# More groups of unread matmuls in the cross-attention units of a fused decoder layer, and another table of them for its last two units

## The chip, the cores and the metric

The kernel runs on one core of one Trainium2 chip. The metric is device time in microseconds (us), the median of several runs. Matmuls and weight loads run on TensorE (PE and PEld in the profile), row maxima and small vector work on VectorE (DVE), exponentials and copies out of PSUM on ScalarE (ACT), elementwise work between SBUF buffers on GpSimd (POOL). SyncE (SP) issues nearly all DMAs.

## The reference

One pre-norm decoder layer over 8 batches of 512 tokens of width 256, 16 heads of width 16:

```python
x = x + attn(layernorm(x), ...)            # rotary self-attention
x = x + xattn(layernorm(x), ctx, ...)      # causal self-attention plus cross-attention, summed, one projection
x = x + ffn(layernorm(x), Wg, w1, w2)      # 16 experts, top 1, capacity 256 tokens each

# xattn
y = softmax(mask(q @ k.T * scale)) @ v                       # causal
y = y + softmax(qc @ kc.T * scale) @ vc                      # against the context
# ffn
gate = softmax(x @ Wg); idx = argmax(gate)
loc = running position of each token within its expert; valid = loc < C
h = relu(dispatched @ w1); out = h @ w2; combined = out[idx, loc] * gate * valid
```

## The kernel before, in words

The attentions are cut into **units**, one attention of one batch each: eight of kind A (rotary, n = 0 to 7), then kind B (causal) and kind C (cross) in turn (B for n = 8, 10, ... 22 and C for n = 9, 11, ... 23). Two units before them only prepare (n = -2, -1), and one behind them (n = 24) only finishes. The units from n = 10 to 21 are the bodies of a loop. A unit with `route=True` also normalises, gates and scatters a finished batch to its expert: those are the **routing units**, n = 11, 13, ... 23, which are all of kind C, and n = 24. Behind the units stand the 16 experts.

Each unit has 32 **slots**, and the order of every engine's work in a slot is written out by hand. On TensorE a slot t is, in this order:

- the product of exponentials and values of three slots back (line 741, tile psO);
- `maxima()`: the scores of 12 slots ahead, query by key, into psS (line 764, for causal ones the masks at lines 772 and 776). DVE takes their negated row maxima (line 1193). psS has three banks, so line 764 waits for the maxima of the slot before (`max_done`). From slot 20 on these scores belong to the next unit;
- `exponents()`: the scores of this slot, key by query, into psK (line 795), with two extra rows that carry the maxima. ACT takes their exponentials (line 1029). Every eighth slot (0, 8, 16, 24) begins a new group of heads, and there line 795 first waits for the DMA that brought the group's maxima (`negmax_in_0` or `negmax_in_1`);
- at slots in the table `WARM_JOB`, some unread matmuls;
- the **jobs** that a table gives this slot: transposes and projections for the unit after the next, values for the next one, output projections, and in routing units two transposes (zT at slots 20 and 21, line 831), the gate's logits (slot 22, line 880) and the counts (slot 25, line 888). They share one bank, psM;
- at slots in the table `WARM_END`, some unread matmuls.

An **unread matmul** (`keep_warm`, line 693) multiplies the first 128 columns of a weight matrix by 512 of its columns into a psK bank that nothing reads before it is overwritten. In `exponents()` the group stands between the scores for the maxima and the wait for the group's maxima, at slot 0 in units A and C and slot 16 in units B:

```python
need(pe, s["exp_done"], b.at("exp_done", w - 1))
keep_warm(psK[:, banks[0], :], b.warm_rows.get(t, 0))
if t % 8 == 0:
    pe.wait_ge(s[f"negmax_in_{g % 2}"], b.at(f"negmax_in_{g % 2}", (0, 32, 32, 64)[g]))
```

The groups of the two tables go to the psK bank that this slot does not use, and wait until all exponentials of the slot before are done.

The normalisation of a routing unit runs on DVE in slot 14 (the small operations of lines 1147 to 1157) and, after one power on POOL (line 1427), in slots 18 and 19 (line 1165). In C units POOL multiplies the result of the attention before by its reciprocal sums (line 1473) once these have come by DMA. The program asks for it in slot 11.

Of the kernel before, what the change touches and what calls it, by code (L numbers as in the profile page):

```python
# [86 lines left out]
            "back": 15, "out": 14},  # L87
}
WARM_JOB = {"A": {5: 2, 7: 2}, "C": {25: 2}}
WARM_END = {"AA": {6: 2}, "AB": {6: 2, 7: 2}, "BB": {6: 2, 7: 2, 30: 2}, "CC": {12: 3, 15: 2}}  # L90
NO_ROW = 65536
NEG = -1e30
LN_EPS = 1e-5
# [7 lines left out]
class Body:  # L101


    def __init__(self, kind, prev, nxt, nx2, n, dn=0, route=False):
        self.kind, self.prev, self.nxt, self.nx2, self.route = kind, prev, nxt, nx2, route
        self.parity = n % 2
        self.fin = prev if prev in ("A", "C") else None
        self.form = "first" if n == -2 else "second" if n == -1 else "end" if kind is None else "A" + nx2 if kind == "A" else kind + kind
        self.slots = SLOTS_OF[self.form]
        self.attn_slot, self.recip_slot, self.norm_slot = (self.slots.get(k) for k in ("attn", "recip", "norm"))  # L110
        self.scatter_slots, self.route_steps, self.chain_slots = (self.slots.get(k, ()) for k in ("scatter", "route", "chain"))
        self.ln_steps, self.load_slots = self.slots.get("ln", ()), self.slots.get("load", ())
        self.warm_job = WARM_JOB.get(kind, {})
        self.warm_end = WARM_END.get(self.form, {})
        self.warm_rows = {16: 3} if kind == "B" else {0: 3}
        self.n, self.dn, self.ahead = n, dn, None
        self.base, self.stride, self.i = {}, {}, 0

# [1483 lines left out]
```

## Time and profile before

| what | value |
|---|---|
| median of 3 runs | 1646.93 us (1642.42 to 1662.5) |
| the profiled execution | 1641.89 us |
| its span (first to last recorded instruction) | 1640.1 us |
| mean granted TensorE clock | 0.965 of full speed |
| TensorE busy (matmuls) | 1443.4 us, 88% of the span |
| VectorE busy | 1211.1 us, 74% |
| ScalarE busy | 1064.8 us, 65% |
| GpSimd busy | 648.6 us, 40% |

The profiled execution is one more run; its time lies 1.79 us above its span. A granted clock of 1.00 is 2.4 GHz and one of 0.50 is 1.2 GHz; a stretch that was at both levels shows a mean. "Idle before" is time in which an engine had nothing running just before an instruction, with what released it behind the arrow.

In the times below, the group of unread matmuls at slot 15 of unit n = 11 starts at 703.57 us.

### The profile page before, as it was taken

How to read it: one execution, taken by the hardware profiler on the slowest of the kernel's cores; microseconds unless marked ns; L12 is line 12 of the kernel's file. 1: busy time of each engine (PE TensorE's matmuls, PEld its weight loads, DVE VectorE, ACT ScalarE, POOL GpSimd, SP SyncE). 2: the span in 40 equal slices, each digit the busy share in tenths (PEclk: the TensorE clock that was granted, in tenths of full speed). 3: DMA queues.
4: the chain of work that ended last, by engine and by line, in shares of the span. 5: the costliest groups of instructions: out<-in, count | busy, mean ns of one | idle time of the engine just before them, and what ended most of it. 6: DMA issues, size and time to landing. Idle time of an engine off the chain costs nothing.

```text
span 1640.1 us, 37863 instructions
## 1 busy us (share of the span) xinstructions
PE 1443.4 (88%) x14610; PEld 650.8 (40%) x14610; DVE 1211.1 (74%) x2434; ACT 1064.8 (65%) x2139; POOL 648.6 (40%) x535
## 2 busy tenths in 40 slices
PE   3799999999999898988988889989889888779997
PEld 1222333332333434334334234334343332259987
DVE  6788878878776776877877877777768677537774
ACT  2477778778777677656766666666767656425652
POOL 2544565456422423226235234342351311225554
PEclk9799999999999999989999999899999999899999
DMA  6445344433323333323323323332233221157771
GB/s 178 114 123 136 110 117 122 118 104 105 90 74 89 99 100 97 94 72 101 89 81 78 100 68 80 99 89 70 80 96 89 67 55 42 48 183 253 255 262 62
DMA packets 119480, 175.82 MB, mean 107 GB/s; under 512 B 26274, under 2 KB 85896, under 8 KB 114697
## 3 DMA queue, kind: packets, MB, share of 16 engines
q1 hardware_dynamic: 111376, 158.50, 34.1%
q0 software_dynamic: 5888, 14.24, 2.6%
q8 instruction: 108, 1.77, 0.5%
q10 hardware_dynamic: 2048, 0.83, 0.2%
q14 instruction: 60, 0.48, 0.1%
HBM read 102.33 MB, written 51.18 MB: 94 GB/s over the span
## 4 chain that ended last, share of the span: by engine, by line
PE 54%; DVE 18%; DMA 9%; ACT 6%; issue 6%; POOL 5%; SPq 2%; POOLq 0%; DVEq 0%; ACTq 0%
PE psO L741 13%; PE psM L466 10%; PE psS L764 9%; DVE negmax L1193 9%; PE psK L466 6%; PE psK L795 6%; ACT probs L1029 4%; PE psS L466 4%; DMA recipB<-recip_scratch 3%; PE psK L693 2%; DMA shared<-shared 1%; DVE xn L1165 1%; PE psM L831 1%; PE psM L880 1%; DMA stack<-mrows 1%
## 5 line engine op out<-in xcount | busy, mean ns | idle before, releaser
L1193 DVE TENSOR_REDUCE negmax<-psS 128x1 f32<-128x512 f32 (+3 forms) x1536 | 869.5, 615 | 266.4 <-PE psS L764 136.0
L1029 ACT ACTIVATE probs<-psK 128x512 f32<-128x512 f32 (+3 forms) x1536 | 753.6, 544 | 306.8 <-PE psK L795 182.7
L741 PE MATMUL psO<-probs,V 128*32 128x256 f32 (+1 forms) x5632 | 444.5, 388 | 21.2 <-ACT U L1021 15.1
L764 PE MATMUL psS<-stack 48*128 48x512 f16 (+3 forms) x1536 | 285.0, 367 | 62.6 <-DVE negmax L1193 57.4
L795 PE MATMUL psK<-stack 50*128 50x512 f16 (+3 forms) x1536 | 278.9, 359 | 23.6 <-DMA stack<-mrows 14.6
L764 PEld LDWEIGHTS psS<-stack 48*128 48x128 f16 x1536 | 74.4, 93 | 377.7 <-DVE negmax L1193 298.8
L741 PEld LDWEIGHTS psO<-probs,V 128*32 128x32 f32 x5632 | 113.3, 108 | 207.8 <-issue 116.3
L795 PEld LDWEIGHTS psK<-stack 50*128 50x128 f16 x1536 | 76.4, 95 | 55.5 <-ACT probs L1029 20.9
L1427 POOL TENSOR_TENSOR rstd<-lnt,minus_half 128x4 f32<-128x4 f32 x24 | 24.6, 1026 | 157.9 <-DVE lnt L1157 157.9
L1553 POOL DMA_INDIRECT out_dram<-stack,put_to x32 | 76.7, 2398 | 17.9 <-issue 9.1
L1441 POOL CAST shared<-shared 128x512 f16<-128x512 f32 x8 | 4.9, 610 | 191.2 <-ACT shared L1051 191.2
L466 PE MATMUL psM<-xT,wx 128*128 128x512 f16 x288 | 74.1, 385 | 5.0 <-POOL xT L1443 2.5
L1443 POOL TENSOR_TENSOR parts<-shared,parts 128x512 f16<-128x512 f32 x64 | 74.0, 1156 | 5.1
L1441 POOL CAST parts<-shared 128x512 f16<-128x512 f32 x64 | 39.1, 612 | 89.4 <-ACT shared L1063 89.4
L831 PE MATMUL psM<-consts,xn 128*128 128x128 f32 x184 | 31.9, 299 | 42.6 <-DVE xn L1165 29.3
L1021 ACT COPY U<-psO 128x512 f32<-128x512 f32 x96 | 56.8, 592 | 15.1 <-PE psO L741 14.6
L693 PE MATMUL psK<-wo 128*128 128x512 f16 x224 | 65.5, 386 | 0.5
L1063 ACT ACTIVATE shared<-psM,bias_qk 128x512 f32<-128x512 f32 x64 | 44.2, 691 | 21.6 <-PE psM L466 21.6
L1473 POOL TENSOR_TENSOR recipB<-packed,recipB 128x1024 f32<-128x1024 f32 x15 | 35.3, 2351 | 57.1 <-DMA recipB<-recip_scratch 57.1
L772 PE MATMUL psS<-halves 64*128 64x128 bf16 x512 | 57.5, 221 | 0.0
L1521 POOL TENSOR_TENSOR shared<-rs,gate_scale 128x4 f32<-128x4 f32 x8 | 1.6, 205 | 139.7 <-DVE scatter_to L1365 139.7
L807 PE MATMUL psK<-halves 64*128 64x128 bf16 x512 | 55.9, 214 | 0.0
(192 smaller groups left out, 2071.3 us busy)
## 6 DMA issues: line engine op xcount, KB each, us to landing
spare<-in_L_ffn_w_dram SPq DMA_DIRECT2D x32, 1024.0 KB, 6.3
parts_scratch<-parts SPq DMA_DIRECT2D x192, 128.0 KB
stack<-parts_scratch SPq DMA_DIRECT2D x96, 256.0 KB, 4.1
stack<-parts_scratch SPq DMA_DIRECT2D x96, 128.0 KB, 4.0
packed<-U SPq DMA_DIRECT2D x192, 64.0 KB
recipB<-recip_scratch SPq DMA_DIRECT2D x48, 256.0 KB
shared<-shared SPq DMA_DIRECT2D x48, 128.0 KB, 2.1
probs<-back_scratch POOLq DMA_DIRECT2D x16, 258.0 KB, 3.2
```

What stands on the lines that cost most here:

```text
L466: mm = nc.tensor.matmul(out, left(x, k), right(y, k), start=(k, x, y) == steps[0], stop=(k, x, y) == steps[-1])
L693: nc.tensor.matmul(out, wo1[:, 0, 0, 0:P], wo1[:, 0, :, :], start=True, stop=True, skip_group_check=True)
L741: mm = nc.tensor.matmul(psO[32 * i:32 * i + 32, q0:q1], v_of(par)[:, kt, 2 * g + i % 2 + PAIRS * (i // 2), :], probs[:, (unit + i % 2) % P ...
L764: mm = nc.tensor.matmul(psS[:, banks[hh], 0:n], stack_of(par, 0)[rows, hp, qt * P:(qt + 1) * P], stack_of(par, 1)[rows, hp, 0:n], start=Tr ...
L772: nc.tensor.matmul(psS[:, banks[hh], n - P:n], unit_a[rows, :], mask_q[rows, :], start=False, stop=False, skip_group_check=True)
L795: mm = nc.tensor.matmul(psK[:, banks[hh], q0:T], stack_of(b.parity, 1)[rows, hp, kt * P:(kt + 1) * P], stack_of(b.parity, 0)[rows, hp, q0: ...
L807: mm = nc.tensor.matmul(psK[:, banks[hh], q0:q0 + P], unit_b[rows, :], mask_k[rows, :], start=False, stop=True, skip_group_check=True)
L1021: nc.scalar.copy(U[:, g % 2, :], psO[:, :]).then_inc(s["av_out"], 1)
L1029: nc.scalar.activation(probs[:, t % P_RING, i, q0:T], psK[:, S_BANKS[t][i], q0:T], ACT.Exp, scale=SM_SCALE / (1 if b.kind == "A" else WSCA ...
L1193: nc.vector.tensor_reduce(negmax[:, g % 2, at:at + 1], psS[:, S_BANKS[u // 2][j], 0:n], AX_X, ALU.max, negate=True).then_inc(s["max_done"], 1)
L1443: nc.gpsimd.tensor_tensor(lo, src, hi, ALU.subtract).then_inc(s[lo_done], 1)
L1553: nc.gpsimd.indirect_dma_start(out=out_rows_dram, out_offset=bass.IndirectOffsetOnAxis(ap=put_to[:, c, st:st + 1], axis=0), in_=eo_sb[c][: ...
```

## The change

Two tables and one selection are edited:

```diff
-WARM_END = {"AA": {6: 2}, "AB": {6: 2, 7: 2}, "BB": {6: 2, 7: 2, 30: 2}, "CC": {12: 3, 15: 2}}
+WARM_END = {"AA": {6: 2}, "AB": {6: 2, 7: 2}, "BB": {6: 2, 7: 2, 30: 2}, "CC": {12: 3, 15: 2, 21: 2},
+            "last": {15: 2, 22: 2}}
...
-        self.warm_end = WARM_END.get(self.form, {})
-        self.warm_rows = {16: 3} if kind == "B" else {0: 3}
+        self.warm_end = WARM_END.get("last" if kind and nx2 is None else self.form, {})
+        self.warm_rows = {"B": {16: 3}, "C": {0: 3, 16: 3}}.get(kind, {0: 3})
```

- Every C unit (eight of them, n = 9 to 23) gets three unread matmuls at slot 16, ahead of the wait for the third group's maxima.
- The C units n = 9 to 21 (seven) get two behind the jobs of slot 21, and these wait until the exponentials of slot 20 are done. In the six routing units among them that is between the second transpose zT and the logits. Unit n = 9 does not route, and its slot 21 has only the transpose of maxima.
- The last two units, n = 22 (B) and n = 23 (C), have nothing more to prepare (`nx2` is None) and get a table of their own. Unit n = 22 loses its groups at slots 6, 7 and 30 (six matmuls) and gets groups at 15 and 22 (four). Unit n = 23 loses the group of three at slot 12, keeps the one at 15 and gets one of two at 22, behind the logits.

Over the run that is 24 + 14 - 2 - 1 = 35 matmuls more. Every line behind the tables moves down by one, so line 795 is 796 afterwards.

TensorE in unit n = 11, slots 15 to 17, before (psO is the product with the values, psS the scores for the maxima, psK from `stack` the scores for the exponentials, psK from `wo` the unread group):

```order
L693 MATMUL psK<-wo 128x512 [waits exp_done]
L693 MATMUL psK<-wo 128x512
L741 MATMUL psO<-probs,V 32x256 x4
L764 MATMUL psS<-stack 128x512 [waits max_done]
L764 MATMUL psS<-stack 128x512
L795 MATMUL psK<-stack 128x512 [waits negmax_in_0,exp_done]
L795 MATMUL psK<-stack 128x512
L741 MATMUL psO<-probs,V 32x256 [waits exp_done]
```

and the same place now:

```order
L694 MATMUL psK<-wo 128x512
L742 MATMUL psO<-probs,V 32x256 x4
L765 MATMUL psS<-stack 128x512 [waits max_done]
L765 MATMUL psS<-stack 128x512
L694 MATMUL psK<-wo 128x512 [waits exp_done]
L694 MATMUL psK<-wo 128x512 x2
L796 MATMUL psK<-stack 128x512 [waits negmax_in_0]
L796 MATMUL psK<-stack 128x512
L742 MATMUL psO<-probs,V 32x256 [waits exp_done]
```

The three new ones stand behind the wait for `max_done` and ahead of the one for `negmax_in_0`.

TensorE in unit n = 11, slots 21 and 22, before (psM from `xn` is the transpose zT, from `negmax` the transpose of the maxima):

```order
L795 MATMUL psK<-stack 128x512 [waits exp_done]
L795 MATMUL psK<-stack 128x512
L867 MATMUL psM<-consts,negmax 16x128 [waits max_done,zT_out]
L831 MATMUL psM<-consts,xn 128x128 [waits ln_out,negmax_rows]
L831 MATMUL psM<-consts,xn 128x128 x3
L741 MATMUL psO<-probs,V 32x256 x4
L764 MATMUL psS<-stack 128x384 [waits max_done]
```

and now:

```order
L832 MATMUL psM<-consts,xn 128x128 [waits ln_out,negmax_rows]
L832 MATMUL psM<-consts,xn 128x128 x3
L694 MATMUL psK<-wo 128x512 [waits exp_done]
L694 MATMUL psK<-wo 128x512
L742 MATMUL psO<-probs,V 32x256 x4
L765 MATMUL psS<-stack 128x384 [waits max_done]
```

The pair comes after the transpose that waits, and before the product of slot 22, its scores and the logits.

TensorE in unit n = 22, slots 15 and 16, now (the first of the groups is new, the second stood there before):

```order
L796 MATMUL psK<-stack 128x128 x2
L804 MATMUL psK<-halves 128x64 x2
L808 MATMUL psK<-halves 128x128 x2
L694 MATMUL psK<-wo 128x512 x2
L742 MATMUL psO<-probs,V 32x256 x4
L765 MATMUL psS<-stack 128x128 x2
L773 MATMUL psS<-halves 128x128 x2
L777 MATMUL psS<-halves 128x64 x2
L694 MATMUL psK<-wo 128x512 x3
L796 MATMUL psK<-stack 128x512 x2
```

Here line 796 with `psK<-stack 128x512` waits for the third group's maxima.

## Rows read from the trace of the kernel before

**Rows 1.** The page: span, engines, granted clock in 40 slices, chain by engine.
```profile
span 1640.1 us, 37863 instructions
PE 1443.4 (88%) x14610; PEld 650.8 (40%) x14610; DVE 1211.1 (74%) x2434; ACT 1064.8 (65%) x2139; POOL 648.6 (40%) x535
PEclk9799999999999999989999999899999999899999
PE 54%; DVE 18%; DMA 9%; ACT 6%; issue 6%; POOL 5%; SPq 2%; POOLq 0%; DVEq 0%; ACTq 0%
```

**Rows 2.** Groups by line: count, busy us, mean ns, idle before, by releaser.
```profile
L1193 DVE TENSOR_REDUCE negmax<-psS 128x1 f32<-128x512 f32 (+3 forms) x1536 | 869.5, 615 | 266.4 <-PE psS L764 136.0 <-PE psS L776 124.9 <-issue 0.3
L764 PE MATMUL psS<-stack 48*128 48x512 f16 (+3 forms) x1536 | 285.0, 367 | 62.6 <-DVE negmax L1193 57.4 <-DMA stack<-parts_scratch 1.3
L693 PE MATMUL psK<-wo 128*128 128x512 f16 x224 | 65.5, 386 | 0.5
```

**Rows 3.** Timeline, line 693: start, us; three at half clock, three at full clock.
```profile
68.88 1.46 PE L693 MATMUL psK<-wo 128*128 128x512 f16 x3
697.50 0.81 PE L693 MATMUL psK<-wo 128*128 128x512 f16 x3
```

**Rows 4.** Slot 15 to next slot 6, n=11 to 21: length; PE, PEld, DVE, ACT, POOL; PEclk.
```profile
703.57:749.44 45.87, 38.53 (x441) 16.89 (x440) 31.25 (x81) 28.57 (x59) 17.49 (x18) 0.89 0.27 80
818.29:861.48 43.19, 35.63 (x442) 15.20 (x440) 31.23 (x85) 28.68 (x59) 16.12 (x18) 0.96 0.27 79
932.03:976.89 44.86, 36.92 (x441) 15.21 (x440) 31.73 (x85) 28.72 (x59) 16.61 (x18) 0.92 0.26 77
1045.54:1090.17 44.63, 39.51 (x441) 17.70 (x439) 29.41 (x85) 28.36 (x59) 13.70 (x16) 0.85 0.26 76
1159.95:1199.84 39.89, 34.16 (x441) 15.13 (x440) 29.15 (x82) 28.37 (x59) 13.59 (x15) 1.00 0.29 83
1269.52:1313.01 43.49, 35.67 (x442) 15.05 (x440) 30.45 (x80) 28.61 (x59) 17.27 (x18) 0.96 0.24 70
```

**Rows 5.** Timeline around slot 16 of unit n = 11, last row n = 15.
```profile
703.29 2.35 POOL L1473 TENSOR_TENSOR shared<-packed,recipB 128x1024 f32<-128x1024 f32 x1 [7.29 <-DMA recipB<-recip_scratch]
703.31 2.35 DVE L1152 TENSOR_SCALAR lnt<-lnt 128x4 f32<-128x4 f32 x1
706.88 0.40 PE L764 MATMUL psS<-stack 48*128 48x512 f16 x2 [2.15 <-DVE negmax L1193]
709.29 1.29 DVE L1193 TENSOR_REDUCE negmax<-psS 128x1 f32<-128x512 f32 x2 [0.67 <-PE psS L764]
...
936.07 0.61 PE L764 MATMUL psS<-stack 48*128 48x512 f16 x2 [2.88 <-DVE negmax L1193]
```

**Rows 6.** Timeline from slot 16 to 20 of unit n = 17.
```profile
1046.32 4.87 DVE L1193 TENSOR_REDUCE negmax<-psS 128x1 f32<-128x512 f32 x8
1047.06 0.39 PE L764 MATMUL psS<-stack 48*128 48x512 f16 x2 [0.35 <-DVE negmax L1193]
1054.56 0.63 PE L831 MATMUL psM<-consts,xn 128*128 128x128 f32 x4 [1.44 <-DVE xn L1165]
```

**Rows 7.** Stretches as in Rows 4: units n = 11 (four), n = 17, n = 23.
```profile
703.70:707.10 3.40, 1.25 (x13) 0.36 (x12) 3.37 (x5) 0.98 (x2) 3.32 (x3) 1.00 0.27 83
707.10:710.50 3.40, 3.40 (x24) 0.53 (x20) 2.73 (x5) 1.87 (x4) 3.32 (x5) 0.51 0.35 105
717.40:720.80 3.40, 1.99 (x23) 1.07 (x23) 1.01 (x4) 1.73 (x5) 0.00 (x0) 1.00 0.09 31
720.80:727.60 6.80, 6.80 (x48) 4.25 (x47) 2.84 (x9) 2.37 (x5) 0.00 (x0) 0.50 0.10 23
...
1055.30:1068.90 13.60, 12.29 (x85) 6.42 (x77) 4.23 (x12) 4.74 (x10) 0.00 (x0) 0.50 0.11 30
...
1389.80:1396.60 6.80, 6.80 (x40) 4.14 (x44) 2.38 (x11) 2.60 (x6) 0.00 (x0) 0.50 0.09 21
```

**Rows 8.** Timeline of slots 21 and 22 of unit n = 11.
```profile
718.85 0.66 PE L831 MATMUL psM<-consts,xn 128*128 128x128 f32 x4 [1.41 <-DVE mrows L1296]
720.58 3.44 PE L880 MATMUL psM<-wg,shared 128*128 128x16 f32 x16
```

**Rows 9.** Timeline, slot 16 of unit n = 22.
```profile
1328.62 0.61 PE L795 MATMUL psK<-stack 50*128 50x512 f16 x2 [2.44 <-DMA stack<-mrows]
```

## The prediction

> **What bounds the kernel now.** I read the page first. TensorE is busy 88% of the span and carries 54% of the chain that ended last, DVE another 18%; the granted clock is full in nearly all slices [rows 1]. So what is added on TensorE is paid unless something there was idle anyway, and a better clock can give back little. The groups by line then show how the two engines hang together: before the scores for the maxima (line 764) TensorE sits idle 62.6 us in all, 57.4 of them for DVE's maxima, and DVE sits idle 266.4 us, nearly all for TensorE's scores [rows 2]. They hand three banks back and forth, so a delay of one soon becomes a delay of the other.
>
> The place of the change is read by comparing like with like. Six routing C units run the same instructions from slot 15 to slot 6 of the next unit, and take 39.89 to 45.87 us [rows 4]. Unit n = 19, at a clock of 1.00 throughout, is the fastest. Two things make the others longer. One is a stall of TensorE at slot 16. In n = 11 POOL's product (line 1473) started as its DMA landed, at 703.29, and a small DVE operation begun at the same moment took 2.35 us, as long as the product; behind it TensorE waited 2.15 us for the maxima, and in n = 15 2.88 [rows 5]. Two more such rows, in units 13 and 21, have 2.38 and 2.27 us. Units 17 and 19 do not: in n = 17 the wait at that place is 0.35 us [rows 6]. The other is the clock at 1.20 GHz, its lower level. In n = 11 it was full up to 707.1, the stretch with the stall, and low in the 3.4 us behind it; full while zT waited for its bank and low for 6.8 us behind that, with the logits in it [rows 7, 8]. In n = 17 it was low for 13.6 us.
>
> The price of a low clock follows from n = 17, which has no stall: 44.63 - 39.89 = 4.74 us longer, at a mean clock of 0.85, which is 2 x 0.15 x 44.63 = 13.4 us at the lower level. That is **0.35 us lost per microsecond of low clock**. A cross-check on n = 11: stall 2.15 and 2 x 0.11 x 45.87 = 10.1 us low, 2.15 + 3.5 = 5.7, against 45.87 - 39.89 = 6.0 [rows 4, 5]. Good enough.
>
> **The change part by part.** Three unread matmuls in a row took 0.81 us at full clock, the last one's 0.38 us of flow-through being hidden in what follows; per matmul that is about 0.22 us, and by the row at half clock, 1.46 us, about 0.42 [rows 3]. So a group of three costs 0.65 or 1.25 us, a group of two 0.43 or 0.84.
>
> *Slot 16, eight C units, 24 matmuls.* They stand behind the wait that is long there (line 764, `max_done`) and ahead of one that shows no idle time in any C unit (line 795, `negmax_in_0`). So they fill no hole. They also come after the stall that goes before the fall of the clock, so I give them no clock either. What they delay: the exponentials on ACT, and the scores of slot 17, for which DVE already waits 0.67 us in n = 11 [rows 5]. In the four units with the stall I therefore take the full price, twice at the low clock (n = 11 and 15, whose clock falls about there) and twice at the full one: 2 x 1.25 + 2 x 0.65 = 3.8. Unit 9, all at full clock and busy: 0.65. In units 17, 19 and 23 DVE runs eight maxima without a gap in 4.87 us, and is itself the limit for four slots; TensorE later waits 1.44 us for xn [rows 6]. Half a group's time may vanish there. Between 0 and 0.65 each I take 0.45: 1.35. Sum **5.8 us**, bounds 3.3 (five units at the full clock, nothing in the other three) and 10.0 (all eight at the low clock).
>
> *Slot 21, seven C units, 14 matmuls.* The added wait (the second exponential of slot 20) is long met, since TensorE has just waited 1.41 us for its bank [rows 8]. Queued behind the pair on TensorE are the product of slot 22, its scores, and the logits, and for these DVE is the one that waits. So the pair is paid: 7 x 0.43 = 3.0, and 0.4 more for one unit in which the clock is low: **3.4 us**, bounds 3.0 and 5.9.
>
> *The clock behind slot 21.* Here the pair can give something. Of the seven routing units with maxima still to do, three lose the clock about the logits: 6.8 us in n = 11, 13.6 in n = 17, 6.8 in n = 23 [rows 7]. In n = 23 the pair comes behind the logits, in which the clock is already down, so nothing is saved. In n = 17 the fall came at 1055.3, behind a wait of 1.44 us in slot 20 [rows 6], ahead of the pair; the pair may shorten the low time, not prevent it. In n = 11 the fall came at 720.8, just where the pair would run. The whole of both is 20.4 us, worth 20.4 x 0.35 = 7.1 us; nothing is the other bound. I take half, **-3.5 us**.
>
> The Trainium skill (TensorE: Matmul & The Clock Gate, Terms) puts the penalty of throttled time at that time times one minus the ratio, half of it here. The comparison of n = 17 with n = 19 gives 0.35, because DVE, ACT and waits take part of the time. By the page's half this term would be -5.1 and the forecast 1.6 us lower; the row decides.
>
> *The last two units.* In n = 22 the new pair at slot 15 stands ahead of a wait of 2.44 us for a DMA [rows 9], which does not hang on it: free, or a loss of 0.43 if that DMA lands early. Its pair at 22 costs 0.43. Six matmuls go, worth 0 to 1.3; since the scores next to them often wait for DVE, I take 0.6. In n = 23 three go (-0.65) and two come, at the low clock there (+0.84) [rows 7]. Sum **0 us**, bounds -1.5 and +1.5. Should the clock fall where groups are gone, 3.4 us of it cost 1.2.
>
> Sum: 5.8 + 3.4 - 3.5 + 0 = **+5.7 us**. Made against the profiled execution, 1641.89, that is 1647.6. The runs shown have a median of 1646.93, 5.0 above it, and spread over 20 us; by that median the sum gives 1652.6. As a base I take the middle of the two, 1644.4, here and for the rivals, and predict **1650 us**. All of this is far within 2% (33 us), about what a measurement of this kernel can tell from no change.
>
> **The rivals.** *The clock is the winner, faster.* Each shift of a few tenths moves where falls of the clock lie. If the pairs hold the clock in the logits of every unit and the slot-16 group helps it back after each stall, the low time from slot 15 to slot 6 over the six units of rows 4, 2 x (0.11 x 45.87 + 0.04 x 43.19 + 0.08 x 44.86 + 0.15 x 44.63 + 0.04 x 43.49) = 37.6 us, goes: -13.2 us. The direct cost with no low clock is 5 x 0.65 + 3 x 0.45 + 3.0 = 7.6. That is -5.6, about 1639 us. For it speaks that n = 19 shows a unit without a fall is possible; against it, that four falls come behind the slot-16 stall, ahead of all added work [rows 5, 7].
>
> *It costs more than its work, slower.* The mechanism is at slot 16. Where DVE has come late by the collision with POOL, it starves for TensorE's scores, and three matmuls more at the low clock keep it starving; the maxima, xn, zT and logits all come 1.25 us later in every unit, and so the idle time that goes before a fall at the logits stays. If all seven routing units have the collision (four of seven do now; three more at some 2.3 us) and the clock gains nothing, it is 10.0 + 5.9 + 7 = 23 us: 1667. With one more collision and values halfway to those bounds, 2.3 + 7.9 + 4.6 = 14.8: 1659. It decides from the point where a fifth unit has it. For it: the start of line 1473 hangs on a DMA. Against: nothing is added in front of slot 15 of a unit, where the collision is made.
>
> *It is absorbed.* Waits on both sides of the pair (1.41 and 1.44 us at zT) and DVE's unbroken run take nearly all of the added time, and the clock is as now: 0 to 2 us, about 1645. Against it is that nearly all of DVE's idle time is for TensorE.
>
> That the groups do not come into the program can be left out: the order of instructions shows all of them.
>
> **How the numbers follow.** The forecast has 0.45, the clock rival 0.22, the slower rival 0.15, absorption 0.18. The range 1638 to 1662 takes in the forecast with its bounds (direct 4.8 to 17.4, clock 0 to -7.1: -2.3 to +17.4), the absorbed case, the clock case at its middle and the milder slower one; the worst of the slower one, and a median moved further by the spread of the runs, are left out. Faster by over 2% would need 33 us, more than twice what the clock has to give: 0.01. Slower by over 2% needs more than the worst sum above: 0.02. Within 2%: 0.97.
>
> **What the profile afterwards would show.** Line 693 (then 694) has 259 psK records instead of 224, give or take a lost one. At slot 16 of C units three of them follow line 764, with no idle time before the scores behind them, and the stretch from slot 16 to 20 is longer by 0.45 to 1.25 us. DVE's idle time before line 1193 grows by some microseconds. Falls of the clock behind slot 16 are still there in units with a long wait at line 764, and those at the logits are fewer or shorter. In unit 22 the wait of 2.44 us is some 2.0. I would be wrong if the clock's low time behind slot 16 fell as well, if it rose where groups were taken away in the last two units, or if the collision of lines 1473 and 1152 became more or less frequent, which moves the time by 2.3 us for each unit with no matmul having cost anything.

## The result, and the profile afterwards

The changed kernel has a median of 1658.97 us (20 runs, 1651.46 to 1673.65), against 1647.71 us (20 runs, 1638.32 to 1670.63) of the kernel before in the same comparison. The ratio is 1.0057, with a 95% interval of 1.003 to 1.0083: **slower by 9.4 us (5 to 13.7)**. By the bound of 2% that is no change, but the interval leaves 1 out. The direction is the forecast's; its sum was +5.7 us. The ratios, here and below, leave out executions more than 1.5% above the fastest of their kernel, the medians do not, so that the two can differ by some microseconds.

The profiled execution took 1655.85 us. First the page of the changed kernel, with span, engines, granted clock in 40 slices and the chain by engine:

```profile
span 1654.1 us, 37925 instructions
PE 1456.7 (88%) x14645; PEld 650.8 (39%) x14645; DVE 1210.6 (73%) x2434; ACT 1064.1 (64%) x2139; POOL 648.4 (39%) x535
PEclk8799999999999999999999989999999899889999
PE 55%; DVE 17%; DMA 7%; issue 7%; ACT 6%; POOL 5%; SPq 2%; POOLq 0%; DVEq 0%; ACTq 0%
```

Against [rows 1] the span is 14.0 us longer, and TensorE has 13.3 us more of busy time. DVE, ACT and POOL have as much as before, to 0.7 us. The groups by line, again of the changed kernel (count, busy us, mean ns, idle before):

```profile
L1194 DVE TENSOR_REDUCE negmax<-psS 128x1 f32<-128x512 f32 (+3 forms) x1536 | 869.8, 615 | 285.0 <-PE psS L765 149.7 <-PE psS L777 129.8 <-issue 0.3
L765 PE MATMUL psS<-stack 48*128 48x512 f16 (+3 forms) x1536 | 286.9, 370 | 63.2 <-DVE negmax L1194 57.4 <-DMA stack<-parts_scratch 2.3
L694 PE MATMUL psK<-wo 128*128 128x512 f16 x259 | 77.1, 393 | 0.3
```

Line 694 has 259 records, 35 more. Before the scores for the maxima TensorE waits for DVE 57.4 us, as in the kernel before [rows 2]: the added matmuls, which stand behind that wait, filled none of it. That the two sums agree to a tenth is chance, since seven further kernels below with nothing added ahead of the wait, and with the product of line 1473 asked for in slot 11 as here, have 56.3 to 63.2 us. DVE's idle time grew by 18.6 us, 13.7 of it waiting for line 765.

The six units of [rows 4], slot 15 to slot 6 of the next (length; PE, PEld, DVE, ACT, POOL; PEclk); the first five, n = 11 to 19:

```profile
708.41:750.53 42.12, 35.37 (x447) 15.48 (x445) 29.71 (x85) 28.33 (x59) 14.03 (x16) 1.00 0.29 81
824.19:866.66 42.47, 36.71 (x447) 15.89 (x445) 29.36 (x84) 28.33 (x59) 13.58 (x15) 0.96 0.27 80
935.78:981.15 45.37, 40.66 (x446) 18.06 (x444) 29.18 (x82) 28.30 (x59) 13.58 (x15) 0.85 0.26 75
1050.13:1095.44 45.31, 36.80 (x447) 15.45 (x445) 32.10 (x85) 28.61 (x59) 16.81 (x18) 0.96 0.26 76
1164.08:1208.70 44.62, 36.78 (x447) 15.44 (x445) 31.45 (x85) 28.44 (x59) 16.04 (x18) 0.96 0.25 74
```

Units 11 and 13, which had the stall at slot 16 and are now without it, are shorter than before; unit 15, also without it now, is 0.5 us longer, at a clock of 0.85; unit 19, which had been the undisturbed one, is 4.7 us longer. So unit by unit the comparison mostly shows where the collision of line 1474 (GpSimd's product, 1473 before) with DVE's small operations fell. The cost of the added work is read where nothing else differs: unit 9, at full clock with no stall. Slots 15 to 17 there, before and then after:

```profile
603.12 0.39 PE L764 MATMUL psS<-stack 48*128 48x512 f16 x2
603.34 0.38 PE L795 MATMUL psK<-stack 50*128 50x512 f16 x2
```

```profile
602.36 0.39 PE L765 MATMUL psS<-stack 48*128 48x512 f16 x2
602.68 0.82 PE L694 MATMUL psK<-wo 128*128 128x512 f16 x3
603.44 0.39 PE L796 MATMUL psK<-stack 50*128 50x512 f16 x2
```

The two scores began 0.22 us apart and now begin 1.08 us apart. Taken from the start of line 795 or 796 in slot 15 to its start in slot 17 (stretches between slots are measured so from here on), 3.47 us became 4.28: **0.81 us for a group of three**, 0.65 for the matmuls by their rate [rows 3] and 0.16 for a group more.

In unit n = 17 the collision is now there, and TensorE's wait ahead of the group is long. DVE's small operation beside POOL's product, and then slot 16:

```profile
1049.23 2.36 POOL L1474 TENSOR_TENSOR shared<-packed,recipB 128x1024 f32<-128x1024 f32 x1 [6.66 <-DMA recipB<-recip_scratch]
1049.44 2.17 DVE L1148 TENSOR_TENSOR lnt<-stats 128x4 f32<-128x4 f32 x1
...
1054.34 0.39 PE L765 MATMUL psS<-stack 48*128 48x512 f16 x2 [3.05 <-DVE negmax L1194]
1054.66 0.82 PE L694 MATMUL psK<-wo 128*128 128x512 f16 x3
1055.42 0.39 PE L796 MATMUL psK<-stack 50*128 50x512 f16 x2
1057.39 1.29 DVE L1194 TENSOR_REDUCE negmax<-psS 128x1 f32<-128x512 f32 x2 [1.32 <-PE psS L765]
```

TensorE stands still for 3.05 us, then does 0.82 us that nobody reads, and DVE behind it stands still for 1.32 us, where it was 0.67 in the same situation [rows 5]. The Trainium skill (SBUF — State Buffer, SBUF: two separate sides) says that DVE and GpSimd share one pair of ports to SBUF: whichever starts first, a GpSimd operation or a DVE one in a two-port mode or (against a GpSimd operation that reads SBUF) with two inputs in SBUF, holds the pair for the whole instruction, and the other is blocked. This trace agrees for the operation above, which has two inputs in SBUF: it started behind the product and took 2.17 us for 128x4 numbers, ending as the product ends, where the same line without a product beside it takes 0.17.

### The profile page after: what moved, and what is told of

Its sections match the earlier page's. It is cut to its first block, busy times and chain, and to the rows that moved or that the text cites. A ratio compares the mean times of both kernels' runs of the same rounds, so it can differ in the third digit from the quotient of the medians.

```text
span 1654.1 us, 37925 instructions
## 1 busy us (share of the span) xinstructions
PE 1456.7 (88%) x14645; PEld 650.8 (39%) x14645; DVE 1210.6 (73%) x2434; ACT 1064.1 (64%) x2139; POOL 648.4 (39%) x535
## 4 chain that ended last, share of the span: by engine, by line
PE 55%; DVE 17%; DMA 7%; issue 7%; ACT 6%; POOL 5%; SPq 2%; POOLq 0%; DVEq 0%; ACTq 0%
PE psO L742 13%; PE psM L467 10%; PE psS L765 9%; DVE negmax L1194 9%; PE psK L467 6%; PE psK L796 6%; ACT probs L1030 4%; PE psS L467 4%; DMA recipB<-recip_scratch 2%; PE psK L694 2%; DVE xn L1166 2%; DMA shared<-shared 1%; PE psM L832 1%; DMA stack<-mrows 1%; PE psM L881 1%
## 5 line engine op out<-in xcount | busy, mean ns | idle before, releaser
L765 PE MATMUL psS<-stack 48*128 48x512 f16 (+3 forms) x1536 | 286.9, 370 | 63.2 <-DVE negmax L1194 57.4
L694 PE MATMUL psK<-wo 128*128 128x512 f16 x259 | 77.1, 393 | 0.3
L1022 ACT COPY U<-psO 128x512 f32<-128x512 f32 x96 | 56.9, 592 | 13.3 <-PE psO L742 12.8
L808 PE MATMUL psK<-halves 64*128 64x128 bf16 x512 | 56.3, 216 | 0.0
```

Source lines behind the costliest of these rows:

```text
L694: nc.tensor.matmul(out, wo1[:, 0, 0, 0:P], wo1[:, 0, :, :], start=True, stop=True, skip_group_check=True)
L765: mm = nc.tensor.matmul(psS[:, banks[hh], 0:n], stack_of(par, 0)[rows, hp, qt * P:(qt + 1) * P], stack_of(par, 1)[rows, hp, 0:n], start=Tr ...
L808: mm = nc.tensor.matmul(psK[:, banks[hh], q0:q0 + P], unit_b[rows, :], mask_k[rows, :], start=False, stop=True, skip_group_check=True)
L1022: nc.scalar.copy(U[:, g % 2, :], psO[:, :]).then_inc(s["av_out"], 1)
```

## The experiments

Each is compared with the kernel before on the same chip. "us" of an effect is the ratio less one, times the median of the kernel before there: 1658.67 us for e1, e2, e3 and e5, 1656.3 for e4, e6, e7 and e8, 1650.67 for e9 to e12. Edits are to the kernel before unless said otherwise.

**e1_slot16 and e11_slot16_again** are one kernel, run on two chips: the slot-16 part alone.

```diff
-        self.warm_rows = {16: 3} if kind == "B" else {0: 3}
+        self.warm_rows = {"B": {16: 3}, "C": {0: 3, 16: 3}}.get(kind, {0: 3})
```

> Only the three unread matmuls at slot 16 of the eight C units are added. Theory of the forecast (they cost TensorE time that nothing hides): +5.8 us, between 3.3 and 10, and in units without a long wait at the scores for the maxima the stretch from slot 15 to 17 is 0.5 to 0.9 us longer than the 3.5 to 3.9 us of the kernel before. Absorption: 0 to 2 us and no longer stretch. Clock rival: 3 to 8 us faster, with fewer falls of the clock behind slot 16.

Measured: 1678.89 us (6 runs), ratio 1.0111 (1.0069 to 1.0152), +18 us (11 to 25).

> The same kernel as the first run of slot 16 alone, which was 18 us slower with 68 us of low clock about the logits of its one profile. If the group at slot 16 brings the falls about the logits on, this profile shows them again (over 40 us) and the time is again 12 to 20 us above the kernel before. If they were chance, the profile shows 10 to 30 us of them and the time is 5 to 9 us above.

Measured: 1664.18 us (12 runs), ratio 1.006 (1.0019 to 1.01), +9.9 us (3.1 to 16.5).

The slot-16 part alone is slower in both runs, and costs at least as much as the whole change; e1 lies above the 3.3 to 10 expected of it. By the traces its direct price is the same 0.81 us in unit 9 in both. Beside it stands a price that comes through the clock, seen cleanly in unit n = 23, where nothing else varies. Slots 15 to 17 and 20 to 26 of it, before and then in e11 (length; PE, PEld, DVE, ACT, POOL; PEclk):

```profile
1375.75:1379.74 3.99, 2.89 (x28) 0.80 (x26) 3.88 (x14) 1.85 (x5) 2.68 (x3) 1.00 0.53 167
1383.73:1399.01 15.28, 12.78 (x101) 6.64 (x102) 4.26 (x17) 8.50 (x17) 0.00 (x0) 0.78 0.04 10
```

```profile
1380.76:1385.54 4.78, 3.70 (x31) 0.93 (x28) 4.20 (x14) 1.79 (x5) 2.90 (x3) 1.00 0.47 144
1389.54:1406.96 17.42, 15.10 (x101) 7.24 (x102) 4.48 (x19) 8.50 (x17) 0.00 (x0) 0.61 0.04 9
```

The group adds 0.79 us where it stands, and 2.14 us more some slots later, with the same instructions: the low clock there lasts 13.7 us instead of 6.8. Those 6.9 us at 0.35 are 2.4, close to the 2.14. The profile of e1 has the same two numbers in this unit (4.78 and 17.41). In the changed kernel, where unit 23 has other groups too, and in e5 below, the low stretch is 6.8 us again, so it does not grow with the amount of work. In e3, which has no group at slot 16, it is 10.2 us. What sets its length is open.

In the other units the two profiles differ. From slot 20 to 26, summed over the routing units 11 to 21, the clock was low for 68.3 us in e1 and 23.9 us in e11 (20.5 before). Two of these stretches in e1:

```profile
721.00:734.70 13.70, 12.39 (x82) 6.31 (x81) 3.81 (x10) 4.68 (x10) 0.00 (x0) 0.50 0.11 31
843.90:857.60 13.70, 12.39 (x89) 6.58 (x85) 5.01 (x16) 4.44 (x11) 0.00 (x0) 0.50 0.09 28
```

At 0.35 us per microsecond 44 us more are 15.5 us, more than the difference of 8 between the two results, whose intervals overlap anyway. One profile can't say what is typical, but the clock is on record for every execution (last part of this section), and it was lower than in the kernel before in both runs. Of the two expectations of e11 the profile meets the one of chance (10 to 30 us of low clock); the time meets neither.

**e5_slot16x12** has 12 matmuls in that group instead of 3:

```diff
+        self.warm_rows = {"B": {16: 3}, "C": {0: 3, 16: 12}}.get(kind, {0: 3})
```

> Slot 16 of the eight C units gets twelve unread matmuls instead of three; nothing else is added. At 0.22 us each at the full clock and nothing hidden this is 8 x 12 x 0.22 = 21 us, up to 40 at the low clock. If the first three are absorbed by waits, the rest is 16 us. If the group helps the clock back after a stall at slot 16, the cost is under 16 us and the low stretches behind slot 16 are at most 3.4 us long.

Measured: 1678.37 us (6 runs), ratio 1.0132 (1.0094 to 1.017), +22 us (15.6 to 28). In unit 9 slots 15 to 17 take 6.22 us, 2.75 above the kernel before; times eight that is 22.0, the measured number. The nine further matmuls cost 1.94 us a unit, 0.216 each, the rate of [rows 3]. By slot 17, nothing of it is hidden. In the profile of e5, its fastest execution, the mean clock was 0.968, and over its six executions 0.959 against 0.960: no loss of clock can be seen with 12, where there is one with 3. Why, is open.

**e6_ahead** moves the three across the wait: ahead of the scores for the maxima, in slot 16 of C units.

```diff
+                    if b.kind == "C" and t == 16:
+                        need(pe, s["exp_done"], b.at("exp_done", 2 * t - 1))
+                        keep_warm(psK[:, S_BANKS[t][0], :], 3)
```

> The three unread matmuls of slot 16 of C units stand ahead of the scores for the maxima instead of behind them, where TensorE waits 2 to 3 us for DVE in units with the collision. Nothing else is added. Theory: in units with the collision they lie in that wait and cost nothing, in the others they cost up to 0.65 us each, so +1 to +3 us in all, 2 to 4 us less than with the group behind. If they hold the clock as well, the falls behind slot 16 go and it is 2 to 4 us faster than the kernel before.

Measured: 1653.71 us (12 runs), ratio 0.9954 (0.992 to 0.9987), -7.6 us (-13.3 to -2.2): **the same 24 matmuls cost less on the other side of one wait.** The intervals of e1 and e11 (3.1 to 25 us) lie wholly above this one. Expected were +1 to +3 us, or 2 to 4 faster should they hold the clock as well. That the kernel is also faster than before is less firm: the medians of all executions, 1653.71 and 1656.3, are only 2.6 us apart. Unit 9 pays nearly the same for the group (4.22 us from slot 15 to 17). The gain lies in units with the collision. The profiled execution took 1661.28 us, 7.6 above the median, so only stretches are read from it. Slots 15 to 20, first before, then e6, in units 11, 13, 15 and 21, the four with a long stall before:

```profile
702.60:713.88 11.28, 9.05 (x74) 2.22 (x72) 10.04 (x20) 6.78 (x13) 8.51 (x9) 0.85 0.39 116
817.32:828.94 11.62, 9.13 (x75) 2.34 (x72) 10.35 (x20) 6.87 (x13) 8.26 (x9) 0.85 0.34 105
931.06:944.46 13.40, 10.44 (x75) 2.37 (x72) 10.93 (x20) 6.92 (x13) 8.85 (x9) 0.75 0.34 107
...
1268.55:1279.97 11.42, 9.06 (x75) 2.20 (x72) 10.24 (x20) 6.81 (x13) 8.51 (x9) 0.85 0.35 107
```

```profile
710.47:719.11 8.64, 8.42 (x77) 2.49 (x75) 8.54 (x20) 6.57 (x13) 6.18 (x8) 1.00 0.39 120
825.21:834.75 9.54, 8.42 (x77) 2.49 (x75) 9.44 (x20) 6.57 (x13) 7.09 (x8) 1.00 0.34 106
937.89:947.87 9.98, 8.42 (x78) 2.49 (x75) 9.88 (x20) 6.57 (x13) 7.64 (x8) 1.00 0.36 112
...
1285.01:1294.87 9.86, 8.42 (x78) 2.48 (x75) 9.76 (x20) 6.58 (x13) 7.52 (x8) 1.00 0.33 103
```

From slot 15 to 20 the clock fell in none of the six units of e6. In the nine profiles in which the product is asked for in slot 11 and nothing stands ahead of the wait (before, after, e1, e2, e3, e5, e7, e11 and e12) it fell in two to four of six each time, 28 of 54. Slots 15 to 20 of the eight C units add up to 79.4 us before, 84.3 after and 73.2 in e6. In its unit 13 the group runs while DVE is held up, and 0.99 us of the wait is left behind it:

```profile
826.92 1.13 DVE L1154 TENSOR_TENSOR lnt<-lnt 128x4 f32<-128x4 f32 x1
827.28 0.82 PE L693 MATMUL psK<-wo 128*128 128x512 f16 x3
829.10 0.39 PE L764 MATMUL psS<-stack 48*128 48x512 f16 x2 [0.99 <-DVE negmax L1196]
```

And TensorE's wait for DVE at line 764, 57.4 us in the two kernels of the change and 56.3 to 63.2 in the seven further ones, is 50.8 here:

```profile
L764 PE MATMUL psS<-stack 48*128 48x512 f16 (+3 forms) x1536 | 285.7, 368 | 57.4 <-DVE negmax L1196 50.8 <-DMA stack<-parts_scratch 2.9
```

Not all is better in this profile. About the logits the clock was low for 41.0 us against 20.5, which is 7 us by the price, so the trace shows where the gain at slot 16 lies, but not how it adds up with the rest.

**e4_norm15 and e8_after_norm15** take the collision away: POOL's product is asked for in slot 15 instead of 11, in the kernel before and in the changed one.

```diff
-  "recip": 8, "norm": 11,
+  "recip": 8, "norm": 15,
```

> The kernel before with one number changed: in C units POOL's product of line 1473 is asked for at slot 15 instead of 11, so it stands behind the power of slot 14 in POOL's order and can't run beside the small DVE operations of the normalisation in slot 14. Theory of the collision: the waits of 2 to 3 us at the scores of slot 16 go in all routing units, and the falls of the clock behind them; the units that had them get 2.3 us plus 1 to 2 us of clock shorter, 10 to 15 us in all if four have it. Rival: the small operations are slow for another reason (or collide with POOL's splits of slots 13 and 15), and the waits stay.

Measured: 1656.56 us (12 runs), ratio 0.9983 (0.9944 to 1.0022), -2.8 us (-9.3 to 3.6).

> The changed kernel with the same number changed to 15. If the added matmuls cost TensorE time whatever the collision does, it is 6 to 9 us above the run of the kernel before with this number. If their cost came from the collision's stalls, at which DVE starves, the two are within 2 us of each other.

Measured: 1649.46 us (12 runs), ratio 0.9959 (0.9925 to 0.9993), -6.8 us (-12.4 to -1.2).

The collision with the operations of slot 14 is gone in both. The tiles' view of e4, all executions of a line (min, median, max ns), with the same lines of the kernel before under it:

```profile
L1147 DVE TENSOR_TENSOR lnt<-stats x24: 164/166/167, 6.8 to 1439.6; 128x4 f32<-128x4 f32 x24
L1152 DVE TENSOR_SCALAR lnt<-lnt x24: 160/164/165, 7.3 to 1440.0; 128x4 f32<-128x4 f32 x24
L1165 DVE TENSOR_SCALAR xn<-X,lnt,rstd x96: 311/407/1967, 9.0 to 1443.4; 128x256 f32<-128x256 f32 x96
```

```profile
L1147 DVE TENSOR_TENSOR lnt<-stats x24: 165/166/2000, 6.7 to 1430.2; 128x4 f32<-128x4 f32 x24
L1152 DVE TENSOR_SCALAR lnt<-lnt x24: 157/163/2354, 7.2 to 1430.7; 128x4 f32<-128x4 f32 x24
L1165 DVE TENSOR_SCALAR xn<-X,lnt,rstd x96: 315/406/1965, 8.9 to 1434.0; 128x256 f32<-128x256 f32 x96
```

The longest of the first two were 2000 and 2354 ns and are now 167 and 165. (The 1965 and 1967 ns of xn lie at the start of both kernels, beside another GpSimd operation.) But a stall has come in elsewhere. Behind the product stands GpSimd's copy of line 1517, and in e4 it runs beside xn in slot 18; here unit 15:

```profile
942.10 2.37 POOL L1473 TENSOR_TENSOR shared<-packed,recipB 128x1024 f32<-128x1024 f32 x1
944.13 1.52 DVE L1165 TENSOR_SCALAR xn<-X,lnt,rstd 128x256 f32<-128x256 f32 x2
944.40 1.11 POOL L1517 COPY shared<-X 128x1024 f32<-128x1024 f32 x1
```

The second xn takes 1.12 us instead of 0.41, in five of six routing units of e4 and in none of e8. Slots 15 to 20 of the C units take 66.9 us in e4 against 79.4, 12.5 less, and the whole kernel gained nothing that can be measured, where 10 to 15 us were expected. Part of it was lost again to the clock: about the logits it was low for 30.7 us against 20.5 in the profile of e4, the longer falls there come ahead of slot 21, and over its executions e4 had a lower clock than the kernel before. With the collision gone in both, the slot-16 group can be read cleanly: 4.28 us in seven units of e8 from slot 15 to 17, 3.47 to 3.52 in six of e4 (unit 23: 4.79 and 4.00). Most of the 0.81 comes back later: from slot 15 to 20 the eight units of e8 take 69.8 us, 2.9 more than in e4, which is 0.8 each in units 9 and 23 about 0.27 in five routing units and nothing in unit 11.

The pair was to show whether the added matmuls cost their time whatever the collision does. They then had to put e8 6 to 9 us above e4. It lies 4.0 us below by the ratios; for the difference of the means, resampling the executions gives -9.7 to 1.8 us. **With the product asked for in slot 15 the change makes nothing slower that can be measured.** The clocks in the last part of this section say why: e8 was 22 us less at the lower clock than e4, worth 7.8 us, which leaves 3.8 us for the added work.

**e2_slot21 and e7_slot21x8** are the pair of slot 21 alone, and with eight matmuls.

```diff
-"CC": {12: 3, 15: 2}}
+"CC": {12: 3, 15: 2, 21: 2}}      # e7: 21: 8
...
+        if kind == "C" and nx2 is None:
+            self.warm_end = {12: 3, 15: 2}
```

> Only the two unread matmuls behind slot 21 of units 9 to 21 are added. Theory of the forecast: 3.4 us of cost less what the clock gives back about the logits, so -1 to +4 us. If the clock gains nothing, +3 to +4 us, and a fall of the clock between slots 20 and 24 still shows in two or three of the routing units. If the clock gains all, no routing unit but the last shows a fall there, and the time is 3 to 4 us lower.

Measured: 1656.23 us (12 runs), ratio 1.0002 (0.9967 to 1.0037), +0.3 us (-5.5 to 6.1).

> Eight unread matmuls behind slot 21 of units 9 to 21 instead of two. Unhidden price: 7 x 8 x 0.22 = 12.3 us. If more of them hold the clock where two do not, no fall of the clock is left between slots 20 and 24 of units 11 to 21, and the cost is some 5 us lower.

Measured: 1663.03 us (12 runs), ratio 1.0033 (0.9995 to 1.0071), +5.5 us (-0.8 to 11.8).

From slot 20 to 22 an undisturbed routing unit took 6.59 us before, 7.03 with the pair and 8.32 with eight: 0.44 for two matmuls, 1.73 for eight, again 0.216 each. Unhidden, the eight had to cost 12.3 us, so their 5.5 lies below that, as expected if they hold the clock, but the interval of 12.6 us leaves that open. In the profile of e2 only 3.4 us are at the lower clock about the logits of units 11 to 21, and in e7 none, against 20.5 before. Here are slots 15 to 20 and 20 to 26 of unit 11 in e2; the logits run at 1.00 just behind a collision:

```profile
715.24:725.10 9.86, 7.67 (x74) 2.27 (x72) 9.76 (x20) 6.57 (x13) 7.53 (x8) 1.00 0.34 105
725.10:740.68 15.58, 11.76 (x145) 6.03 (x143) 9.18 (x29) 8.53 (x18) 1.16 (x1) 1.00 0.16 44
```

That points to the matmuls at slot 21 holding the clock. With the product asked for in slot 11, the four profiles that have them (the changed kernel, e2, e12 and e7) show 17.1, 3.4, 3.4 and 0 us, the six without 13.7 to 68.3. With the product in slot 15 the profile without has 30.7 us and the three with them 17.1 to 37.5, so there the profiles don't show it. The times show no gain over the kernel before.

**e9_pair_norm15 and e10_four_norm15** are e2 with the product asked for in slot 15, with two and with four matmuls at slot 21.

```diff
+  "recip": 8, "norm": 15,
+"CC": {12: 3, 15: 2, 21: 2}}      # e10: 21: 4
```

> The kernel before with POOL's product asked for at slot 15 and with the pair behind slot 21 of units 9 to 21, without the group at slot 16 and without the new table of the last two units. If slot 16's group is what makes the changed kernel slower, this is 5 to 7 us below the changed kernel with the product at slot 15, so 0.7 to 0.9% below the kernel before. If the group at slot 16 helps there (the clock), it is no better than that kernel's 0.4%.

Measured: 1643.34 us (12 runs), ratio 0.9982 (0.9948 to 1.0017), -3.0 us (-8.6 to 2.8).

> As the run with the pair and the product at slot 15, with four unread matmuls behind slot 21 instead of two. They cost 0.43 us more in each of seven units, 3.0 us. With eight there, no fall of the clock was left about the logits, with two some were. If four hold it as eight did, the low time saved (5 us a unit where it falls, in one or two units) pays for them and the time is that of the pair or 1 to 3 us lower; if not, 3 us higher.

Measured: 1650.61 us (12 runs), ratio 0.9995 (0.9959 to 1.0032), -0.8 us (-6.8 to 5.3).

Neither can be told from before. e9 was expected 0.7 to 0.9% below the kernel before if the slot-16 group is what costs the time; it is 0.18% below, and e8, which has the group, 0.41%: with the product in slot 15 the group shows no price. In the two profiles the clock was low about the logits for 30.7 and 37.5 us, no less than in e4 without the pair, and the longer falls come ahead of slot 21, too early for it.

**e3_last** has only the new table of the last two units.

```diff
-        self.warm_end = WARM_END.get(self.form, {})
+        self.warm_end = {15: 2, 22: 2} if kind and nx2 is None else WARM_END.get(self.form, {})
```

> Only the last two units get their new table: six matmuls gone and four come in unit 22, three gone and two come in unit 23. Theory of the forecast: no change, within 1.5 us. A rival: the groups taken away from unit 22 (slots 6, 7, 30) or unit 23 (slot 12) held the clock, and falls at those places now cost 1.2 to 2.4 us each.

Measured: 1657.53 us (12 runs), ratio 0.9984 (0.9941 to 1.0026), -2.7 us (-9.8 to 4.3): no difference that can be measured.

**e12_after_minus16** is the changed kernel without its slot-16 group.

```diff
-        self.warm_rows = {"B": {16: 3}, "C": {0: 3, 16: 3}}.get(kind, {0: 3})
+        self.warm_rows = {16: 3} if kind == "B" else {0: 3}
```

> The changed kernel without its group at slot 16: the pair behind slot 21 and the new table of the last two units stay. If the loss is slot 16's, this is level with the kernel before, within 3 us. If the pair or the table cost as well, it is 3 to 6 us above.

Measured: 1653.17 us (12 runs), ratio 1.0 (0.9963 to 1.0037). Without the slot-16 group the loss is gone; the other two parts together are worth 0 us, give or take 6.

**The clock over many executions.** Profiles are single executions, but the mean granted clock is on record for each one. Twice its shortfall from 1, times the span, is the time at the lower clock. In the executions that the ratios use:

| run | what it has | mean clock, kernel before | us at the lower clock, more than before | worth at 0.35, us |
|---|---|---|---|---|
| e1 | slot 16 | 0.950, 0.960 | +38 (24 to 53) | 13 |
| e11 | slot 16 | 0.957, 0.962 | +16 (6 to 26) | 6 |
| e5 | slot 16, twelve | 0.959, 0.960 | +6 (-10 to 22) | 2 |
| e6 | slot 16, ahead | 0.963, 0.960 | -10 (-21 to 1) | -4 |
| e2 | slot 21 | 0.961, 0.960 | 0 (-10 to 10) | 0 |
| e7 | slot 21, eight | 0.963, 0.960 | -11 (-20 to -2) | -4 |
| e12 | slot 21, last units | 0.963, 0.962 | -3 (-12 to 6) | -1 |
| e4 | product in slot 15 | 0.956, 0.960 | +13 (2 to 24) | 5 |
| e9 | product in slot 15, slot 21 | 0.960, 0.962 | +6 (-3 to 15) | 2 |
| e10 | the same, four | 0.961, 0.962 | +2 (-7 to 10) | 1 |
| e8 | product in slot 15, whole change | 0.963, 0.960 | -9 (-20 to 2) | -3 |

The brackets are 95% intervals from resampling the executions. (The price of 0.35 holds here roughly: among the executions of the kernel before, the time rises by 0.31 to 0.55 us per us of low clock on the three chips.) e3 has no difference (0, -9 to 10). Two things show. The group of three at slot 16 alone lowers the clock, in both runs; take the worth off, and 5 us of e1 and 4 of e11 are left for the work itself. And the low time that e1, e11 and e4 have more is not seen, or not clearly (e9), in the kernels that have matmuls at slot 21 besides: e8 lies 22 us below e4 (8 to 36). The changed kernel has 0.961 in the mean of its 20 executions; the clocks of the kernel before in that comparison are not on record, but on the three chips of the experiments it has 0.960 to 0.962. It did not lose the clock that its slot-16 part loses alone. That the pair at slot 21 does this is the plain reading, but no run is the changed kernel without just the pair.

## Why the prediction was right, and where its sizes were off

The direction held, +5.7 us lies inside the measured 5 to 13.7, and 1658.97 us inside the range of 1638 to 1662, though 9 us above the forecast and at the very figure of the milder slower rival (1659). That the sum came this near owes something to luck: alone, the group at slot 16 loses clock worth 6 to 13 us, for which the sum has nothing, and it holds only because that loss is not there in the whole change. Step by step:

- **"So they fill no hole" (slot 16): right, and this is the loss.** e1 and e11 have it alone, e12 lacks only it, and e6 has the same matmuls ahead of the wait. The sum said 5.8 us (3.3 to 10.0). By the stretch at full clock it is 8 x 0.81 = 6.5 up to slot 17, and e5 bears out the rate. Up to slot 20, 2.9 us of it are left between e4 and e8. (Between the kernel before and after it is 4.9, but kernels without the group differ by more than that among themselves there, 75.5 to 87.1 us.) Of the whole kernels' times, 4 to 5 us are left once the clock's part is taken off. The direct term was of the right size. What was wrong is "so I give them no clock either": alone, the group costs 16 to 38 us of full clock, 6 to 13 us of time (e1, e11). Wrong in the other direction was the group itself, 0.65 instead of 0.81. The 0.45 taken for units 17, 19 and 23 was too low for unit 23, which paid 0.79 from slot 15 to 17 (3.99 to 4.78) and still had 0.80 by slot 20; most routing units without the collision had 0.27 left there (e4 to e8).
- **The pair at slot 21: right, a little high.** 3.4 us forecast, six units at 0.44 = 2.6 measured. Unit 9 paid 0.48 from slot 20 to 22 and had it back by slot 24 in the changed kernel and in e12, but not in e2 and e8.
- **The clock behind slot 21, -3.5 us: the term that was mis-sized.** From slot 20 to 26 the profile of the changed kernel was at the lower clock for 17.1 us, against 20.5 before: 3.4 us less, worth 1.2. Over the executions there is no gain over the kernel before either (e2: 0, -10 to 10 us of low clock; e12: -3, -12 to 6). I had taken half of a possible 7.1 with no row that showed the pair doing anything. What the pair seems to do is to keep the clock that the slot-16 group would lose, and that loss I had not seen. Put 2.6 and -1.2 in place of 3.4 and -3.5, and 6.5 for 5.8, and the sum is 7.9, against the measured 9.4 (5 to 13.7).
- **The last two units, 0:** e3 (-9.8 to 4.3) does not contradict it. The risk I named, a fall where groups were taken away, did come in unit 23. Slots 0 to 12 of that unit had no such fall before; in the changed kernel and in e3 the clock was low there for 3.4 us, and the unit was 2.2 and 3.3 us longer. e8 and e12 have the same table and no fall there, so this is a risk, not a price. In unit 22 the wait at slot 16 is 0.96 us, shorter than the 2.44 of [rows 9] by more than the pair's 0.43, but it proves nothing: the wait is 1.72 to 4.87 us in the kernels with the old table, and 4.43 in e12 with the new one.

```profile
1339.17 0.39 PE L796 MATMUL psK<-stack 50*128 50x512 f16 x2 [0.96 <-DMA stack<-mrows]
```

- **"The collision ... became more or less frequent"**, the first thing named as able to upset it, happened, in part: four of six units before (11, 13, 15, 21), three after (17, 19, 21). Nothing in the change touches POOL or the DMA, and profiles of one kernel differ in it as well: a wait of over 2 us at slot 16 shows in all six units of e1 and in four of e11, the same kernel.
- **The rival "costs more than its work"** is not excluded. Its threshold, a fifth unit with the collision, was not reached in the profiled execution, and what it claimed of DVE is there only at a fraction of its price (1.32 us of starving in unit 17). But its time is the measured one, the slot-16 group alone did cost more than its work, and with the collision taken away (e4 and e8) the change costs nothing that can be measured. How much of the 9.4 us needs the collision, no run says.
- **The clock rival** is excluded by the interval (it wanted -5.6), **absorption** too (0 to 2 us against 5 to 13.7).
- The base: the medians of the larger comparison lie some us higher than mine, the kernel before at 1647.71 instead of 1644.4; with it the same sum gives 1653.4.

Not settled: why the slot-16 group alone loses the clock, why e1 lost more of it than e11, the same kernel on another chip, and whether it is the pair at slot 21 that keeps it in the changed kernel. Units 10 and 12, of kind B, where the program was not changed, were 4.8 us longer each in the profile of the changed kernel (57.4 and 56.8 us instead of 52.6 and 51.9), with falls behind a wait of TensorE for ACT ahead of the scores of slot 17 (2.73 and 2.06 us). Unit 10 takes 52.5 to 53.5 us in seven of the fourteen profiles and 56.4 to 58.3 in the other seven, with and without the change. That part of the 14.0 us between the two profiled spans belongs to the pair of executions, and is not a cost of the change.

## What to carry to other kernels

Put filler for TensorE ahead of a long wait, not behind it: 24 matmuls behind the wait for the maxima made this kernel slower by 0.6% and 1.1% in two runs, the same 24 ahead of it did not. Before placing it, read for each wait of the slot how long it is and which of them comes first on the engine. Price such a group twice, by its work and by the clock: here the work was some 5 us and the clock 6 to 13, and the second part was not there in the kernel that had matmuls further on as well. One profile can't give the second price, as single profiles of one kernel differ threefold in low clock at one place; take the clock of many executions. And where two engines hand a few banks back and forth, look for the small operation that a neighbour stretches tenfold, but follow the neighbour: when GpSimd's product was moved, the copy behind it came to stretch another operation.

## What the runs showed of the hardware that was not expected

- Stretches of low clock 13.7 us long at the same place of unit after unit in the profile of e1, and a third of that time in the profile of the same kernel on another chip.
- With 0.8 us added at slot 16 of unit 23 a low stretch some five slots later was twice as long, 13.7 us instead of 6.8, in two runs alike, and with twelve matmuls at the same place (2.73 us) it was not.
- Over six and eight executions a group of three unread matmuls at slot 16 lowered the mean clock from 0.960 to 0.950 and from 0.962 to 0.957 (two chips). In the two kernels that have matmuls at slot 21 as well, the changed one and e8, it was 0.961 and 0.963.
- Three short matmuls (0.82 us) ahead of the wait for the maxima, and the clock fell from slot 15 to 20 in no unit of six; without them in 28 of 54.
- A DVE operation on 128x4 numbers that normally takes 0.16 us takes up to 2.35 us when it starts together with a GpSimd product of 128x1024 numbers; one on 128x256 numbers (xn) takes 1.12 us instead of 0.41 beside a GpSimd copy of 128x1024. At slot 14 it cost the units that had it some 2.3 us of TensorE's time, and yet taking it away there gave -2.8 us (-9.3 to 3.6) for the kernel, not 10 or more, with 13 us (2 to 24) more at the lower clock.
